# Expert up products with weight blocks stationary and 128 tokens moving, and the routing weight moved into the token rows

## The chip, the cores and the metric

The kernel runs on one core of one Trainium2 chip. The metric is the device time of one execution in microseconds (us), and the figure quoted for a kernel is the median over its runs. The profile comes from one further execution of the same program; its span runs from the first to the last instruction.

## The reference

The network works on 4 sequences of 512 tokens, 2,048 tokens of width 128, in six steps: a feed-forward block, a causal attention with 16 heads, the feed-forward block again, a mixture of experts, a second attention, and the mixture of experts again. Everything is float32. Only the mixture of experts is touched here:

```
def _L1_ffn_ref(X, Wg, bg, W1, W2, W3):          # E = 8 experts, top S = 2, H = 512
    logits = einsum('btd,de->bte', X, Wg) + bg
    topv, topi = top_k(logits, S)
    w = softmax(topv, axis=-1)
    xs = X[:, :, None, :] * w[..., None]
    out = X
    for e in range(E):
        h = silu(einsum('btsd,dh->btsh', xs, W1[e])) * einsum('btsd,dh->btsh', xs, W3[e])
        y = einsum('btsh,hd->btsd', h, W2[e])
        out = out + where(topi == e, y, 0).sum(axis=2)
```

The routing weight `w` multiplies the token row before both up products, so it stands inside the silu and once more in the other factor.

## The kernel before

Matrix products run on TensorE in float16. Each float32 operand is split into a high and a low half, and a product is three matmuls (high by high, high by low, low by high), which `split_mm` issues. Each weight is scaled by `W_UP` = 64 before it is split.

A mixture of experts is the function `moe(m)`, written once in each engine's program: m = 0 follows the first attention, m = 1 the second. The 4,096 pairs of token and expert are sorted by expert into tiles of 128 rows, padded so that each tile has one expert. There are `ETILES` = 46 tiles in two halves of `HT` = 23. The loop `run_tiles` goes over iterations t = 0 to 48 and calls up to four stages in each, with lags 0, 1, 2 and 3, and then `carried(m, t)`. The stages of tile t:

- Lag 0. GpSimd has fetched the tile's 128 token rows from memory with an indirect DMA (`gather`, L883) into `XG`, a ring of `XRING` = 4 buffers; the buffer is free again once TensorE has transposed it. TensorE transposes the rows (`turned_token`, L2130) into PSUM bank 0, ScalarE writes the high half (`token_high`, L1153), VectorE the low half (`token_low`, L1699).
- Lag 1. TensorE makes the two up products (`up`, L1746 to L1748, through `split_mm`): the token halves are stationary and 512 columns of the expert's weights move. The result stands tokens by hidden units in bank 1 (W1) and bank 2 (W3). ScalarE applies silu with the tile's row weights `wup` as scale (`gate`, L1161). VectorE multiplies the other product by `wup` and by the silu into `G32` (`product`, L1709).
- Lag 2. TensorE transposes the four 128 by 128 blocks of `G32` (`turned_product`, L2155) into bank 3 or 4, because the down product needs hidden units on the partitions. ScalarE writes the high half `GH` (`product_high`, L1167), VectorE the low half `GL` (`product_low`, L1715).
- Lag 3. TensorE makes the down product with twelve matmuls (`down`, L2167 to L2169): a 128 by 128 block of `GH` or `GL` is stationary, 128 columns of the expert's `E2` move. ScalarE scales the result (`result`, L1175), and GpSimd scatters the rows to memory (`scatter`, L891), eight iterations behind its gathers (`OUT_LAG` = 8).

Which expert a tile belongs to is known only at run time. TensorE's program reads the offsets of eight tiles at a time from SBUF into registers (`load_offsets`, called behind `up` at iterations that come five times in each `moe` after the start), and the address of each weight slice is worked out in registers: `ds(e, H)` in `up`, `ds(e + f * D, D)` in `down`, for the high and the low weights.

`carried(m, t)` puts other work between the tiles: the last turn of the attention ahead of them, for m = 0 the end of the second feed-forward block, the routing of the second half of the tokens (`routed`), for m = 0 transposes of the second attention's weights (`second_turned`, L2063), and the first turn of the next attention. Every engine works through its own program in order. `GRING` = 3 is the number of buffers of `GH` and `GL`.

Of the kernel before, what the change touches and what calls it, by code (L numbers as in the profile page):

```python
# [31 lines left out]
def macaron_block(nc: bass.Bass, ins, out, phases):  # L32
    tokens = ins["L0_attn_tokens"]
    NB, SEQ, D = tokens.shape
    P = 128
# [32 lines left out]
    with ctx:  # L68
# [296 lines left out]

        s_t_ps = sem("t_ps")
# [6 lines left out]
        s_gt_ps = sem("gt_ps")  # L373
# [7 lines left out]
        s_act_done = sem("act_done")  # L381

# [525 lines left out]
        def _(act):  # L908
# [237 lines left out]
            def moe(m):  # L1146
# [8 lines left out]
                def gate(t, w):  # L1155
                    if t % HT == 0:
                        act.wait_ge(s_r_weight, PARTS * m + t // HT + 1)
                    act.wait_ge(s_a_ps, w + 1)
                    if t >= 2:
                        act.wait_ge(s_g32_rdy, w - 1)  # L1160
                    a_.activation(SA[:, t % 2, :], ps[:, 1, :], ACT.Silu, scale=wup[:, t:t + 1]).then_inc(s_a_sb, 1)  # L1161

                def product_high(t, w):
                    act.wait_ge(s_gt_ps, w + 1)
                    if t >= GRING:
                        act.wait_ge(s_y_ps, w - GRING + 1)
                    a_.activation(GH[:, t % GRING].rearrange("p a b -> p (a b)"), ps[:, 3 + t % 2, :], ACT.Copy  # L1167
# [28 lines left out]
        def _(dve):  # L1196
# [389 lines left out]
            def homes_half(m, h):  # L1586
# [16 lines left out]
                v_.tensor_scalar(wup[:, at], wrow, 1.0 / W_UP, None, ALU.mult).then_inc(s_r_weight, 1)  # L1603
# [91 lines left out]
            def moe(m):  # L1695

                def token_low(t, w):
                    dve.wait_ge(s_t_hi, w + 1)
                    v_.tensor_tensor(XTt[:, t % 2, 1], ps[:, 0, 0:P], XTt[:, t % 2, 0], ALU.subtract  # L1699
                                     ).then_inc(s_t_lo, 1)  # L1700

                def product(t, w):
                    if t % HT == 0:
                        dve.wait_ge(s_r_weight, PARTS * m + t // HT + 1)
                    dve.wait_ge(s_a_sb, w + 1)
                    dve.wait_ge(s_b_ps, w + 1)
                    if t >= 2:
                        dve.wait_ge(s_gt_ps, w - 1)
                    v_.scalar_tensor_tensor(G32[:, t % 2, :], ps[:, 2, :], wup[:, t:t + 1], SA[:, t % 2, :], ALU.mult,  # L1709
                                            ALU.mult).then_inc(s_g32_rdy, 1)  # L1710

                def product_low(t, w):
                    g = t % GRING
                    dve.wait_ge(s_g_hi, w + 1)
                    v_.tensor_tensor(GL[:, g].rearrange("p a b -> p (a b)"), ps[:, 3 + t % 2, :],  # L1715
# [19 lines left out]
        def _(pe):  # L1735
# [376 lines left out]
            def moe(m):  # L2112
# [13 lines left out]
                def turned_token(t, w):  # L2126
                    pe.wait_ge(s_xg_in[t % XRING], moved(m, t % XRING, t + 1))
# [4 lines left out]
                def up(t, w):  # L2132
                    k, e = t % 2, offsets[t]
                    pe.wait_ge(s_t_lo, w + 1)
                    if t >= 1:
                        pe.wait_ge(s_a_sb, w)
                    split_mm(ps[:, 1, :], XTt[:, k, 0], XTt[:, k, 1], E1h[:].rearrange("p e h -> p (e h)")[:, ds(e, H)],
                             E1l[:].rearrange("p e h -> p (e h)")[:, ds(e, H)], s_a_ps)
                    if t >= 1:
# [57 lines left out]
```

## Time and profile before

| | us |
|---|---|
| median of 3 runs | 949.98 (949.64 to 950.70) |
| the profiled execution, its own time | 951.23 |
| its span | 949.4 |
| TensorE busy | 846.3 (89%) |
| VectorE busy | 788.4 (83%) |
| GpSimd busy | 744.6 (78%) |
| ScalarE busy | 646.6 (68%) |

TensorE is PE in the rows, its weight loads PEld, VectorE DVE, ScalarE ACT and GpSimd POOL. Instructions of TensorE overlap, so their durations add up to more than the time they take; what a matmul takes in a stream is the distance from one start to the next. Register arithmetic, register loads and waits are not shown as instructions. The two mixtures of experts run from about 357 to 508 us and from about 801 to 938 us of the span.

### The profile page before, as it was taken

To read this page: it belongs to the slowest core of one execution; us is meant where nothing else is said; L and a number is where in the kernel's file an instruction comes from. 1 tells how busy PE (TensorE), PEld (TensorE's weight loads), DVE (VectorE), ACT (ScalarE), POOL (GpSimd) and SP (SyncE) were. 2 spreads that over 40 slices of the span, in tenths; PEclk is the share of its full clock that TensorE was granted. 3 is DMA by queue.
4 is the path that set the end of the run, shared out by engine and by line. 5 is a ranking of instruction groups with operands and counts; after the bars stand their busy time and mean duration, and the time that the engine had idled before them with its cause. 6 is when DMAs were issued, how large, how long until landed. Compare 5 with 4: busy or idle time off the path is not lost.

```text
span 949.4 us, 32967 instructions
## 1 busy us (share of the span) xinstructions
PE 846.3 (89%) x12648; PEld 598.3 (63%) x12648; DVE 788.4 (83%) x2498; ACT 646.6 (68%) x1119; POOL 744.6 (78%) x685
## 2 busy tenths in 40 slices
PE   5779999999999867999997889999999995999994
PEld 3356675676666655776764566676777774576673
DVE  6769999989999976897776799898999987786673
ACT  6658797888787745766774667776676763566662
POOL 6849999999898956776653899988898985677762
PEclk9889999999999998999997999999999997999997
DMA  5122423242422341223111222133322231122232
GB/s 161 46 62 42 91 50 87 48 96 47 92 47 46 53 124 37 66 51 93 49 35 62 30 41 47 41 64 52 53 58 53 53 63 43 49 48 52 95 72 84
DMA packets 123516, 58.92 MB, mean 62 GB/s; under 512 B 106978, under 2 KB 112866, under 8 KB 123364
## 3 DMA queue, kind: packets, MB, share of 16 engines
q1 hardware_dynamic: 116128, 43.68, 21.3%
q0 software_dynamic: 5888, 12.07, 5.1%
q8 instruction: 106, 1.74, 0.8%
q10 hardware_dynamic: 1348, 1.05, 0.4%
q14 instruction: 46, 0.38, 0.2%
HBM read 22.44 MB, written 9.18 MB: 33 GB/s over the span
## 4 chain that ended last, share of the span: by engine, by line
PE 49%; DVE 19%; POOL 18%; issue 5%; ACT 5%; DMA 3%; SPq 0%; POOLq 0%; DVEq 0%; ACTq 0%
POOL arena L832 11%; PE ps L1746 6%; PE ps L1748 6%; PE ps L1747 6%; DVE ps L1347 5%; PE ps L1925 5%; PE ps L2155 4%; POOL arena L830 3%; PE ps L1899 2%; PE ps L2168 2%; PE ps L2167 2%; PE ps L2169 2%; PE ps L1958 2%; DVE arena L1371 1%; DMA T<-arena 1%
## 5 line engine op out<-in xcount | busy, mean ns | idle before, releaser
L832 POOL TENSOR_TENSOR arena<-arena 128x1024 f16<-128x1024 f32 x190 | 347.2, 1828 | 61.3 <-ACT arena L1028 51.3
L1020 ACT ACTIVATE arena<-ps,lift 128x1024 f32<-128x1024 f32 (+1 forms) x192 | 187.2, 975 | 114.4 <-PE ps L1935 103.9
L1347 DVE CUSTOM_DVE_ANT_0 ps<-ps,mask_qk 128x512 f32<-128x512 f32 (+3 forms) x512 | 238.6, 517 | 15.3 <-PE ps L1899 14.3
L1925 PE MATMUL ps<-arena 64*128 64x512 f16 (+3 forms) x1536 | 149.0, 299 | 13.9 <-ACT arena L1020 10.5
L883 POOL DMA_INDIRECT arena<-x_rows,arena x92 | 90.9, 989 | 57.0 <-PE ps L2130 21.9
L1958 PE MATMUL ps<-arena 128*128 128x65 f16 x1280 | 124.8, 195 | 5.5 <-DVE arena L1366 2.1
L1958 PEld LDWEIGHTS ps<-arena 128*128 128x128 f16 x1280 | 116.1, 97 | 18.8 <-issue 12.2
L891 POOL DMA_INDIRECT y_rows<-arena x92 | 91.0, 989 | 43.5 <-issue 22.7
L1959 PE MATMUL ps<-arena 128*128 128x64 f16 x1280 | 124.2, 193 | 0.0
L1960 PE MATMUL ps<-arena 128*128 128x65 f16 x1280 | 123.8, 193 | 0.0
L1959 PEld LDWEIGHTS ps<-arena 128*128 128x128 f16 x1280 | 117.3, 99 | 0.3 <-issue 0.3
L1960 PEld LDWEIGHTS ps<-arena 128*128 128x128 f16 x1280 | 117.3, 98 | 0.0
L830 POOL CAST arena<-arena 128x1024 f16<-128x1024 f32 x124 | 103.0, 831 | 0.0
L1925 PEld LDWEIGHTS ps<-arena 64*128 64x128 f16 x1536 | 55.0, 94 | 62.3 <-ACT arena L1020 34.8
L1709 DVE SCALAR_TENSOR_TENSOR arena<-ps,arena 128x512 f32<-128x512 f32 x92 | 68.8, 748 | 25.2 <-ACT arena L1161 23.4
L1899 PE MATMUL ps<-arena 64*128 64x512 f16 (+3 forms) x512 | 68.3, 304 | 21.1 <-DVE arena L1347 19.1
L1167 ACT ACTIVATE arena<-ps 128x512 f16<-128x512 f32 x92 | 54.9, 597 | 40.6 <-PE ps L2155 40.6
L1161 ACT ACTIVATE arena<-ps,arena 128x512 f32<-128x512 f32 x92 | 63.2, 687 | 27.7 <-PE ps L1748 26.7
L1715 DVE TENSOR_TENSOR arena<-ps,arena 128x512 f16<-128x512 f32 x92 | 63.3, 688 | 20.3 <-ACT arena L1167 19.8
L1347 DVE DVE_READ_ACCUMULATOR2_ANT arena<- 128x1 f16 x512 | 73.1, 143 | 0.0
L1354 DVE SCALAR_TENSOR_TENSOR arena<-ps,arena 128x512 f16<-128x512 f32 x64 | 43.8, 684 | 31.7 <-ACT arena L1041 31.7
L2167 PE MATMUL ps<-E2h,arena 128*128 x368 | 67.3, 219 | 1.8 <-ACT arena L1175 1.1
(283 smaller groups left out, 2609.7 us busy)
## 6 DMA issues: line engine op xcount, KB each, us to landing
stage<-in_L_ffn_W SPq DMA_DIRECT2D x4, 1024.0 KB, 5.6
arena<-y_rows SPq DMA_DIRECT2D x14, 256.0 KB, 3.8
x_rows<-XN SPq DMA_DIRECT2D x8, 256.0 KB, 2.3
arena<-x_rows,arena POOLq DMA_INDIRECT x92, 3.0
y_rows<-arena POOLq DMA_INDIRECT x92
stage<-in_L_attn_Wkv SPq DMA_DIRECT2D x2, 512.0 KB, 8.5
arena<-arena SPq DMA_TRANSPOSE x64, 2.3
T<-arena SPq DMA_TRANSPOSE x64, 3.1
```

The lines of the kernel that those rows point to most:

```text
L830: g.tensor_copy(PH[:, b, :, cols], P32[:, :, cols]).then_inc(s_ph_pool, 1)
L832: g.tensor_tensor(PL[:, b, :, cols], P32[:, :, cols], PH[:, b, :, cols], ALU.subtract).then_inc(s_pl, 1)
L883: g.indirect_dma_start(XG[:, t % XRING, :], None, x_rows[t // HT], bass.IndirectOffsetOnAxis(ap=row_i[:, 0, t:t + 1], axis=0)).then_inc(s_ ...
L891: g.indirect_dma_start(y_rows, bass.IndirectOffsetOnAxis(ap=row_i[:, 1, t:t + 1], axis=0), YS[:, t % YRING, :], None).then_inc(s_y_out[t % ...
L1020: a_.activation(P32[:, :, UNIT_AT[u]:UNIT_AT[u] + UNIT_W[u]], ps[:, 4:6, 0:UNIT_W[u]], ACT.Exp, bias=lift[:]).then_inc(s_ex_p, 1)
L1347: v_.tensor_tensor_reduce(ps[:, 2 + x, at:at + w], ps[:, 2 + x, at:at + w], mask_qk[:, CH - w:CH], 1.0, NEG, ALU.add, ALU.max, accum_out=M ...
L1899: ins_ = mm(ps[:, 2 + x, at:at + (i + 1) * P], QKh[rows, r, 0, i * P:(i + 1) * P], QKh[rows, r, 1, 0:(i + 1) * P], start=(n_ == 0), stop=( ...
L1925: mm(ps[:, 4 + x, at:at + w], keys, queries, start=(n_ == 0 and part == 0), stop=False)
L1958: mm(ps[:, bank, c:c + DH + 1], ph_, VH[:, r, k, x, 0:DH + 1], start=(k == 0), stop=False)
L1959: mm(ps[:, bank, c:c + DH], ph_, VL[:, r, k, x, :], start=False, stop=False)
L1960: ins_ = mm(ps[:, bank, c:c + DH + 1], pl_, VH[:, r, k, x, 0:DH + 1], start=False, stop=(k == i))
L2167: mm(dst, GH[:, g, f, :], wh, start=(f == 0), stop=False)
```

## The change

The up products are turned round. Blocks of 128 by 128 weights are now stationary and the 128 tokens of the tile move, so the result comes out as hidden units by tokens, four blocks side by side in a bank, and `turned_product` is gone. A row weight would then lie along the free dimension of the product, so it is multiplied into the token rows instead, before their transpose, by a new VectorE instruction (`scaled`). `wup` now holds the weight times `W_UP`. The two up products have two banks each (1 and 3, 2 and 4) in turn. `product_high` and `product_low` read `G32` in SBUF where they read the transposed copy in PSUM.

```diff
+        def a_bank(t):
+            return 1 + 2 * (t % 2)
+        def b_bank(t):
+            return 2 + 2 * (t % 2)
...
 # ScalarE
                 def gate(t, w):
-                    if t % HT == 0:
-                        act.wait_ge(s_r_weight, PARTS * m + t // HT + 1)
                     act.wait_ge(s_a_ps, w + 1)
...
-                    a_.activation(SA[:, t % 2, :], ps[:, 1, :], ACT.Silu, scale=wup[:, t:t + 1]).then_inc(s_a_sb, 1)
+                    a_.activation(SA[:, t % 2, :], ps[:, a_bank(t), :], ACT.Silu, scale=1.0 / (W_UP * W_UP)).then_inc(s_a_sb, 1)
                 def product_high(t, w):
-                    act.wait_ge(s_gt_ps, w + 1)
+                    act.wait_ge(s_g32_rdy, w + 1)
...
-                    a_.activation(GH[:, t % GRING].rearrange("p a b -> p (a b)"), ps[:, 3 + t % 2, :], ACT.Copy
+                    a_.activation(GH[:, t % GRING].rearrange("p a b -> p (a b)"), G32[:, t % 2, :], ACT.Copy
                                   ).then_inc(s_g_hi, 1)
...
 # VectorE
-                v_.tensor_scalar(wup[:, at], wrow, 1.0 / W_UP, None, ALU.mult).then_inc(s_r_weight, 1)
+                v_.tensor_scalar(wup[:, at], wrow, W_UP, None, ALU.mult).then_inc(s_r_weight, 1)
...
+                def scaled(t):
+                    if t % HT == 0:
+                        dve.wait_ge(s_r_weight, PARTS * m + t // HT + 1)
+                    dve.wait_ge(s_xg_in[t % XRING], moved(m, t % XRING, t + 1))
+                    xg = XG[:, t % XRING, :]
+                    v_.tensor_scalar(xg, xg, wup[:, t:t + 1], None, ALU.mult).then_inc(s_xg_scaled, 1)
...
                 def token_low(t, w):
+                    if t == 0:
+                        scaled(0)
                     dve.wait_ge(s_t_hi, w + 1)
                     v_.tensor_tensor(XTt[:, t % 2, 1], ps[:, 0, 0:P], XTt[:, t % 2, 0], ALU.subtract
                                      ).then_inc(s_t_lo, 1)
+                    if t + 1 < ETILES:
+                        scaled(t + 1)
 
                 def product(t, w):
...
                     if t >= 2:
-                        dve.wait_ge(s_gt_ps, w - 1)
-                    v_.scalar_tensor_tensor(G32[:, t % 2, :], ps[:, 2, :], wup[:, t:t + 1], SA[:, t % 2, :], ALU.mult,
-                                            ALU.mult).then_inc(s_g32_rdy, 1)
+                        dve.wait_ge(s_g_lo, w - 1)
+                    v_.scalar_tensor_tensor(G32[:, t % 2, :], ps[:, b_bank(t), :], 1.0 / (W_UP * W_UP), SA[:, t % 2, :],
+                                            ALU.mult, ALU.mult).then_inc(s_g32_rdy, 1)
 
                 def product_low(t, w):
                     g = t % GRING
                     dve.wait_ge(s_g_hi, w + 1)
-                    v_.tensor_tensor(GL[:, g].rearrange("p a b -> p (a b)"), ps[:, 3 + t % 2, :],
+                    v_.tensor_tensor(GL[:, g].rearrange("p a b -> p (a b)"), G32[:, t % 2, :],
                                      GH[:, g].rearrange("p a b -> p (a b)"), ALU.subtract).then_inc(s_g_lo, 1)
...
 # TensorE
                 def turned_token(t, w):
-                    pe.wait_ge(s_xg_in[t % XRING], moved(m, t % XRING, t + 1))
+                    pe.wait_ge(s_xg_scaled, w + 1)
...
                 def up(t, w):
                     k, e = t % 2, offsets[t]
                     pe.wait_ge(s_t_lo, w + 1)
-                    if t >= 1:
-                        pe.wait_ge(s_a_sb, w)
-                    split_mm(ps[:, 1, :], XTt[:, k, 0], XTt[:, k, 1], E1h[:].rearrange("p e h -> p (e h)")[:, ds(e, H)],
-                             E1l[:].rearrange("p e h -> p (e h)")[:, ds(e, H)], s_a_ps)
-                    if t >= 1:
-                        pe.wait_ge(s_g32_rdy, w)
-                    split_mm(ps[:, 2, :], XTt[:, k, 0], XTt[:, k, 1], E3h[:].rearrange("p e h -> p (e h)")[:, ds(e, H)],
-                             E3l[:].rearrange("p e h -> p (e h)")[:, ds(e, H)], s_b_ps)
+                    for bank, wh, wl, free, ready in ((a_bank(t), E1h, E1l, s_a_sb, s_a_ps),
+                                                      (b_bank(t), E3h, E3l, s_g32_rdy, s_b_ps)):
+                        if t >= 2:
+                            pe.wait_ge(free, w - 1)
+                        for f in range(HB):
+                            at = ds(e + f * P, P)
+                            split_mm(ps[:, bank, f * P:(f + 1) * P], wh[:].rearrange("p e h -> p (e h)")[:, at],
+                                     wl[:].rearrange("p e h -> p (e h)")[:, at], XTt[:, k, 0], XTt[:, k, 1],
+                                     ready if f == HB - 1 else None)
...
-                def turned_product(t, w):
-                    k = t % 2
-                    pe.wait_ge(s_g32_rdy, w + 1)
-                    if t >= 2:
-                        pe.wait_ge(s_g_lo, w - 1)
-                    for f in range(HB):
-                        ins_ = nc.tensor.transpose(ps[:, 3 + k, f * P:(f + 1) * P], G32[:, k, f * P:(f + 1) * P], ident[:])
-                    ins_.then_inc(s_gt_ps, 1)
...
-                run_tiles(m, (turned_token, up, turned_product, down), carried)
+                run_tiles(m, (turned_token, up, None, down), carried)
```

## Rows read from the trace of the kernel before

**Rows 1.** Busy time by stage; columns: PE, PEld, DVE, ACT, POOL, PEclk, DMA share.

```profile
397.00:434.00 37.00, 35.16 (x349) 25.34 (x345) 32.97 (x103) 22.96 (x53) 28.14 (x28) 1.00 0.22 51
845.00:928.00 83.00, 80.68 (x737) 57.98 (x735) 57.84 (x115) 54.03 (x126) 58.47 (x60) 1.00 0.27 69
```

**Rows 2.** The chain that ended last, 840 to 940 us, by line.

```profile
by line: PE ps L2155 16.1%; PE ps L1746 15.6%; PE ps L1747 15.1%; PE ps L1748 15.1%; PE ps L2168 8.3%; PE ps L2167 8.1%; PE ps L2169 7.8%; DMA arena<-y_rows 4.6%; PE ps L2130 4.3%; issue 3.4%; DMA y_rows<-arena 2.2%; POOL y_rows L891 1.0%; 
```

**Rows 3.** Timeline of PE, one tile of the second mixture; start, duration, line.

```profile
856.12 0.28 PE L2130 MATMUL ps<-ident,arena 128*128 128x128 f32 x1
856.24 0.38 PE L1746 MATMUL ps<-E1h,arena 128*128 x1
...
857.53 0.60 PE L2155 MATMUL ps<-ident,arena 128*128 128x128 f32 x4
857.97 0.22 PE L2167 MATMUL ps<-E2h,arena 128*128 x1
...
858.64 0.28 PE L2130 MATMUL ps<-ident,arena 128*128 128x128 f32 x1
```

**Rows 4.** Timeline of PEld: token transposes of tiles 4 and 45, both mixtures.

```profile
374.31 0.14 PEld L2130 LDWEIGHTS ps<-ident,arena 128*128 128x128 f32 x1
...
497.12 0.14 PEld L2130 LDWEIGHTS ps<-ident,arena 128*128 128x128 f32 x1
...
817.23 0.14 PEld L2130 LDWEIGHTS ps<-ident,arena 128*128 128x128 f32 x1
...
927.69 0.14 PEld L2130 LDWEIGHTS ps<-ident,arena 128*128 128x128 f32 x1
```

**Rows 5.** Timeline of PEld: a down product that follows a wait.

```profile
503.04 0.10 PEld L2167 LDWEIGHTS ps<-E2h,arena 128*128 128x128 f16 x1 [0.56 <-issue]
...
503.30 0.10 PEld L2167 LDWEIGHTS ps<-E2h,arena 128*128 128x128 f16 x1
503.39 0.10 PEld L2168 LDWEIGHTS ps<-E2l,arena 128*128 128x128 f16 x1
503.42 0.10 PEld L2169 LDWEIGHTS ps<-E2h,arena 128*128 128x128 f16 x1
503.54 0.10 PEld L2167 LDWEIGHTS ps<-E2h,arena 128*128 128x128 f16 x1
...
503.95 0.10 PEld L2169 LDWEIGHTS ps<-E2h,arena 128*128 128x128 f16 x1
```

**Rows 6.** Timeline of PEld behind a reload of the offsets.

```profile
871.06 0.42 PEld L2155 LDWEIGHTS ps<-ident,arena 128*128 128x128 f32 x4 [1.26 <-issue]
...
872.21 0.10 PEld L2169 LDWEIGHTS ps<-E2h,arena 128*128 128x128 f16 x1
872.30 0.14 PEld L2130 LDWEIGHTS ps<-ident,arena 128*128 128x128 f32 x1
872.55 0.10 PEld L1746 LDWEIGHTS ps<-E1h,arena 128*128 128x128 f16 x1
```

**Rows 7.** Timeline of POOL, 894 to 898 us.

```profile
894.39 0.97 POOL L883 DMA_INDIRECT arena<-x_rows,arena  x1 [0.30 <-PE ps L2130]
895.66 0.99 POOL L891 DMA_INDIRECT y_rows<-arena  x1 [0.30 <-issue]
896.96 0.97 POOL L883 DMA_INDIRECT arena<-x_rows,arena  x1 [0.30 <-PE ps L2130]
```

**Rows 8.** Timelines of DVE and POOL around 410 us.

```profile
409.77 1.22 DVE L1538 TENSOR_TENSOR arena<-row_no,arena 128x1024 f16<-128x1024 f16 x1
...
410.12 1.71 POOL L883 DMA_INDIRECT arena<-x_rows,arena  x1 [0.30 <-issue]
```

**Rows 9.** The page's lines of VectorE's low half and of a gather's landing.

```profile
L1715 DVE TENSOR_TENSOR arena<-ps,arena 128x512 f16<-128x512 f32 x92 | 63.3, 688 | 20.3 <-ACT arena L1167 19.8
...
arena<-x_rows,arena POOLq DMA_INDIRECT x92, 3.0
```

**Rows 10.** Busy time, 510 to 520 us, in the columns of the first group.

```profile
510.00:520.00 10.00, 7.17 (x47) 3.19 (x47) 6.00 (x22) 3.52 (x6) 1.27 (x2) 0.63 0.38 118
```

More of the change, by code:

```diff
@@ L364, in macaron_block @@
         s_xg_in = [sem("xg_in0"), sem("xg_in1"), sem("xg_in2"), sem("xg_in3")]
+        s_xg_scaled = sem("xg_scaled")
         s_t_ps = sem("t_ps")
@@ L372, in macaron_block @@
         s_g32_rdy = sem("g32_rdy")
-        s_gt_ps = sem("gt_ps")
         s_g_hi = sem("g_hi")
@@ L1700, in token_low @@
                                      ).then_inc(s_t_lo, 1)
+                    if t + 1 < ETILES:
+                        scaled(t + 1)
                 def product(t, w):
-                    if t % HT == 0:
-                        dve.wait_ge(s_r_weight, PARTS * m + t // HT + 1)
                     dve.wait_ge(s_a_sb, w + 1)
```

## Prediction

> **What bounds the kernel now.** I read the page's chain first. It is spread over the whole network, and only the two mixtures of experts are touched, so I went to the busy times by stage. In the plain stretch of the second mixture PE is busy 80.68 of 83 us and no other engine above 58.47 [rows 1]. The chain of that stretch is PE almost alone: the product transposes of L2155 hold 16.1% of it, the up products 46%, the down product 24% [rows 2]. The timeline then gives one tile: token transpose 0.12 us, up products from 856.24 to 857.53, 1.29 us, product transposes 0.44, down product 0.67, together 2.52 us from one token transpose to the next [rows 3]. GpSimd is hardly slower a bound: gather and scatter follow each other at 1.27 and 1.30, 2.57 us a tile [rows 7]. From the token transpose of tile 4 to that of tile 45 it takes 122.8 us in the first mixture and 110.5 in the second, 41 tiles each, 3.00 and 2.69 us a tile [rows 4]. What lies above 2.52 is carried work and the reloads of the offsets. In the routing stretch of the first mixture DVE is busy 32.97 of 37 us and bounds along with PE [rows 1].
>
> **What the change removes from PE.** The four transposes, 0.44 us a tile, and the wait for `G32` ahead of them. Six matmuls of 512 columns become 24 of 128. In the down product a matmul of 128 columns with a weight load of its own takes (858.64 - 857.97) / 12 = 0.056 us [rows 3], so 24 take 1.34 in place of 1.29. Array time falls from 2.52 to 0.12 + 1.34 + 0.67 = 2.13 us a tile. Here a rule of the Trainium skill speaks against the change ("TensorE: Matmul & The Clock Gate", section on the back-to-back issue gap): in a real kernel a stream of weight loads and 128-column matmuls is put at about 81 ns each. By it the 24 would take 1.94 us and the tile, down product included, about 3.0. The 0.056 us row disagrees, and I do not use the rule.
>
> **What it adds to PE's program, and this decides.** A weight slice's address depends on the tile's expert and is worked out in registers between the matmuls. In the plain tile this costs nothing, because the six long up matmuls let PE's program run ahead of the array. One place shows its own pace: the down product behind a wait at 503.04 us, with nothing issued ahead. The loads of a group of three start 0.12 us, 0.09 and 0.03 apart (503.42 to 503.54, 503.30 to 503.39, 503.39 to 503.42): a new offset `e + f * D` with the address of the high slice, then the address of the low slice, then a load whose address is known. A group takes 0.24 us where the array needs 0.17, and the first eleven steps of the twelve loads take 0.91 [rows 5]. Behind a reload of the offsets the pace shows again: 0.09 from the last load of a down product to the token transpose and 0.25 from there to the first up load [rows 6].
>
> After the change the tile has 12 such groups in place of 4, and no long matmul behind which they could be issued. I sum its issue: token transpose 0.09; first up group 0.25 + 0.09 + 0.03 = 0.37; the other seven 0.24 each if every `e + f * P` is worked out anew, 0.21 if one that is already known is used again (0.09 + 0.09 + 0.03), 1.47 to 1.68; the down product's first group, behind its waits, 0.27, the other three 0.63 to 0.72. That makes 2.83 to 3.13 us; I take 3.0. It is above the array's 2.13, GpSimd's 2.57 and what DVE needs for a tile, so PE's issue sets the pace. Nothing hides it.
>
> **The sum.** 41 tiles at 3.0 are 123.0 us in each mixture. Five reloads of the offsets: each shows as 1.26 us without a load [rows 6]; between nothing more and 1.3 is on the path, I take 1.2, so 6.0. Carried matmuls are issued at 0.03 each: in the second mixture the routing's 65, 2.0 us; in the first mixture about 190, 5.7, and 3.0 us of array time that issue does not cover. This last is an estimate: the next attention's first turn has six matmuls of 512 columns at 1.29 / 6 = 0.215 and twelve of 128 at 0.056, 2.0 us, the feed-forward's down products 64 of 128, 3.6 us; they lie in three iterations, each of which covers 3.0 - 2.13 = 0.87. Second mixture: 131.0 against 110.5, 20.5 more. First: 137.7 against 122.8, 14.9 more. The first four tiles wait on the attention's end, and behind tile 45 three iterations lose the transposes and gain issue; I put both at nothing, within 1 us either way. Together 35.4. The profiled execution took 951.23 us (its span of 949.4 and 1.8 around it), 1.25 above the median of the runs; 951.2 + 35.4 = 986.6, and on the scale of the runs 985.4. I say 985.
>
> **The other edits.** `scaled` adds one DVE instruction a tile. None of its kind and size is in these rows. The nearest is the low half of 512 columns, 0.69 us [rows 9]; a quarter of it, 0.17, is the lower bound, 0.97 the upper, if it must wait out a whole GpSimd instruction [rows 7]. I take 0.3, near the shorter end, as it has 128 columns: 12 us of DVE in each mixture, inside the 0.5 us that the tile gets longer. It also puts the landing of a gather (3.0 us [rows 9]) into DVE's queue ahead of `product` and `product_low`; at 3.0 us a tile the gathers run ahead and the wait is empty. If PE were as fast as its array, DVE would wait there in every tile. `gate` and `product` change a scale only; `product_high` reads as many elements from SBUF; both at nothing. The second set of banks lets `up` start two tiles ahead of its readers, which PE doesn't need while it issues late.
>
> **Rivals.** *GpSimd's pace, faster.* If address work were hidden (say the eight new groups cost no more than their matmuls), gathers and scatters would set 2.57 us a tile. Issue decides from 2.57 us on. Second mixture: 41 x 2.57 = 105.4, 5.1 less, and about 6 less at the end, since a token transpose would follow its gather by the landing's 3.0 us instead of trailing by the ring. First mixture: the routing stretch stays with DVE, the plain 21 tiles give some 6. That is 17 less, 933 us. For it speaks that PE is now the longest queue; against it the 0.24 us group.
>
> *The shared reader.* A gather that began at 410.12 us, while a DVE instruction with two SBUF inputs ran, lasted 1.71 us instead of 0.97, and that DVE instruction ended at 410.99 [rows 8]. `product_low` (0.69 us [rows 9]) gets two SBUF inputs, once a tile. Where GpSimd bounds, each tile could lose up to about 0.33: 2.9 us a tile, which eats most of the 17, 947 us. At 3.0 us a tile GpSimd has 0.4 to spare, and it costs nothing. The Trainium skill says the same of this pair ("SBUF — State Buffer", rules on the shared port pair: a VectorE instruction with two SBUF inputs blocks a GpSimd instruction that reads SBUF); the row agrees, with 0.74 us lost once.
>
> *The slow clock.* PE's granted clock is 1.00, its upper level (2.4 GHz), in both stretches [rows 1], and 0.63 at 510 us, where PE waits for whole microseconds [rows 10]. A late issue makes many short gaps, not long ones. If the clock fell to its lower level (1.2 GHz), the 36 short matmuls would take 0.111 each, 4.2 us a tile: 82 tiles by 1.2 more, about 1,085 us.
>
> **How the numbers follow.** Issue bound 0.74, GpSimd's pace 0.14, GpSimd with the shared reader 0.06, slow clock 0.04, something without effect 0.02. The likeliest case's own range is 968 to 1,006: 2.83 to 3.13 us a tile is 14 us down and 11 up, and reloads and carried work are 6 us either way. To hold 8 in 10 the range must take in the shared reader's 947, and it leaves out the fast rival and the slow clock: 945 to 1,008. About 0.2% is what a measurement of this kernel can tell from no change. Faster by more than that: 0.18 (the fast rival and most of the shared reader's). Within it: 0.03. Slower: 0.79.
>
> **What the changed profile would show.** Right: no L2155; in the plain stretch a token transpose every 2.9 to 3.1 us; weight loads of the up products 0.12, 0.09 and 0.03 apart, not 0.056 even; "issue" high in the chain; DVE, ACT and POOL each with idle time in every tile; POOL waiting for L2130 before its gathers. The fast rival would show loads 0.056 apart and POOL without a wait, 2.57 us a tile, with DVE idle ahead of `scaled` until the gather lands. The shared reader would show scatters or gathers of 1.1 to 1.6 us. The prediction falls if address work costs the array nothing when the weights are the stationary side, or if fewer addresses are worked out than I counted.

## The result and the profile after

The changed kernel takes 1006.19 us (median of 5 runs, 1001.9 to 1010.58) against 949.64 for the kernel before in the same session; the ratio is 1.0607, with a 95% interval of 1.0577 to 1.0637. A second comparison, in a later session, gave 1.0605 (1.0582 to 1.0629). The change makes the kernel slower by 6%. The profiled execution took 1010.58 us, its span is 1008.7; the spans are 949.4 and 1008.7, 59.3 apart; the medians are 56.5 apart.

In the kernel after, L2145 is the token transpose, L1761 to L1763 the three matmuls of a group in `up`, L2174 to L2176 those of `down`, L891 the gather and L899 the scatter; on VectorE L1708 is `scaled`, L1714 `token_low`, L1724 `product` and L1730 `product_low`, on ScalarE L1167 is `gate` and L1181 `result`.

The token transposes of tiles 4 and 45 after, in the timeline of PE's weight loads, against those of [rows 4]:

```profile
376.24 0.14 PEld L2145 LDWEIGHTS ps<-ident,arena 128*128 128x128 f32 x1
...
523.18 0.14 PEld L2145 LDWEIGHTS ps<-ident,arena 128*128 128x128 f32 x1
...
845.21 0.14 PEld L2145 LDWEIGHTS ps<-ident,arena 128*128 128x128 f32 x1
...
986.34 0.14 PEld L2145 LDWEIGHTS ps<-ident,arena 128*128 128x128 f32 x1
```

The 41 tiles take 146.9 us in the first mixture and 141.1 in the second, 24.1 and 30.7 more than [rows 4]. That is 54.8 of the 59.3 us. The rest, 4.5, lies outside these stretches (1.9 of it ahead of tile 4 of the first mixture, 1.9 between the mixtures).

Busy time by stage after: both stages of the first mixture, both of the second, and the plain tiles alone; columns as in [rows 1].

```profile
400.00:441.00 41.00, 39.64 (x504) 32.51 (x503) 34.13 (x113) 19.41 (x49) 26.13 (x26) 1.00 0.19 42
441.00:523.20 82.20, 73.98 (x872) 62.57 (x871) 51.15 (x115) 43.02 (x104) 44.41 (x46) 0.96 0.18 49
...
878.00:986.30 108.30, 100.66 (x1171) 82.31 (x1168) 62.15 (x146) 48.74 (x124) 59.32 (x60) 0.97 0.21 53
886.00:908.90 22.90, 22.73 (x264) 18.24 (x262) 12.58 (x29) 10.95 (x28) 13.72 (x14) 1.00 0.20 43
```

A reader who stops here sees a PE that is busy 22.73 of 22.90 us in the plain tiles and may take the array for the bound. The chain of these tiles says the same, with nearly nothing under "issue" (critical chain, 886 to 909 us):

```profile
by line: PE ps L1761 30.8%; PE ps L1763 15.1%; PE ps L2175 14.9%; PE ps L1762 13.6%; PE ps L2174 12.8%; PE ps L2176 7.3%; PE ps L2145 4.9%; issue 0.7%
```

It isn't the array. A matmul's busy time in this trace runs from its start to its end, and the 36 short ones overlap; how closely they follow each other can only be read from the loads. DVE is busy 55% of these tiles, ACT 48%, POOL 60%: all three wait, and PE waits for none of them (its matmuls show no wait at all from 886 to 909 us). This is one plain tile (892.56 to 895.78 us, 3.22 us) in the timeline of the loads; left out are the groups that look like their neighbours.

```profile
892.56 0.14 PEld L2145 LDWEIGHTS ps<-ident,arena 128*128 128x128 f32 x1
892.81 0.10 PEld L1761 LDWEIGHTS ps<-arena,E1h 128*128 x1
892.82 0.10 PEld L1762 LDWEIGHTS ps<-arena,E1h 128*128 x1
892.97 0.10 PEld L1763 LDWEIGHTS ps<-arena,E1l 128*128 x1
893.11 0.10 PEld L1761 LDWEIGHTS ps<-arena,E1h 128*128 x1
893.13 0.10 PEld L1762 LDWEIGHTS ps<-arena,E1h 128*128 x1
893.20 0.10 PEld L1763 LDWEIGHTS ps<-arena,E1l 128*128 x1
893.35 0.10 PEld L1761 LDWEIGHTS ps<-arena,E1h 128*128 x1
...
894.62 0.10 PEld L1763 LDWEIGHTS ps<-arena,E3l 128*128 x1
894.84 0.10 PEld L2174 LDWEIGHTS ps<-E2h,arena 128*128 128x128 f16 x1
894.97 0.10 PEld L2175 LDWEIGHTS ps<-E2l,arena 128*128 128x128 f16 x1
895.01 0.10 PEld L2176 LDWEIGHTS ps<-E2h,arena 128*128 128x128 f16 x1
...
895.68 0.10 PEld L2176 LDWEIGHTS ps<-E2h,arena 128*128 128x128 f16 x1
895.78 0.14 PEld L2145 LDWEIGHTS ps<-ident,arena 128*128 128x128 f32 x1
```

A group of three starts every 0.24 us (893.11 to 893.35), where the array needs 0.17. The loads of L1761 and L1763, each with an address of its own, come late (0.14 to 0.15 and 0.07 us behind the load before them); that of L1762, on the address that L1761 has just used, comes 0.01 to 0.02 us behind it. The seven tiles from 886.08 to 908.9 take 3.25 us each.

Around a reload of the offsets the same view shows, for the down product's first load and the ones behind it:

```profile
910.90 0.10 PEld L1763 LDWEIGHTS ps<-arena,E3l 128*128 x1
913.20 0.10 PEld L2174 LDWEIGHTS ps<-E2h,arena 128*128 128x128 f16 x1 [2.21 <-issue]
```

2.30 us in place of the 0.22 of a plain tile (894.62 to 894.84). Before the change it was 1.26 without a load [rows 6]. Behind this one the clock is at its lower level (1.2 of 2.4 GHz) for most of the next 4.2 us (granted clock 0.59 in the second row; busy time by stretch, the columns as above):

```profile
911.00:913.30 2.30, 0.21 (x4) 0.10 (x1) 1.29 (x2) 0.36 (x1) 0.70 (x1) 1.00 0.19 61
913.30:917.50 4.20, 4.20 (x46) 4.10 (x46) 0.70 (x3) 1.61 (x4) 1.96 (x2) 0.59 0.07 19
```

The engines' waits in the plain tiles, 886 to 909 us (total, times, longest), say who waits for whom:

```profile
DVE arena L1724 <- ACT arena L1167: 8.5, 7, 1.3
POOL arena L891 <- PE ps L2145: 6.8, 7, 1.5
ACT arena L1181 <- PE ps L2176: 6.7, 7, 1.1
ACT arena L1167 <- PE ps L1763: 5.1, 7, 0.8
```

POOL waits about 1 us for the token transpose before each gather, in seven of seven tiles; before the change the gathers of [rows 7] begin 0.30 us behind the scatter, the distance that stands between any two starts, and so do 19 of the 22 gathers from 850 to 908 us (0.30 to 0.36).

### The profile page after: what moved, and what is told of

It is laid out like the page before. It is cut to its first block, busy times and chain, and to the rows that moved or that the text cites. A ratio compares the mean times of both kernels' runs of the same rounds, so it can differ in the third digit from the quotient of the medians.

```text
span 1008.7 us, 36649 instructions
## 1 busy us (share of the span) xinstructions
PE 892.3 (88%) x13936; PEld 665.0 (66%) x13936; DVE 801.6 (79%) x2590; ACT 633.1 (63%) x1119; POOL 755.1 (75%) x685
## 4 chain that ended last, share of the span: by engine, by line
PE 55%; POOL 18%; DVE 14%; issue 5%; ACT 5%; DMA 2%; SPq 0%; POOLq 0%; ACTq 0%; DVEq 0%
POOL arena L840 11%; PE ps L1761 11%; PE ps L1763 7%; PE ps L1762 6%; PE ps L1940 5%; DVE ps L1353 4%; PE ps L2175 4%; PE ps L2174 3%; POOL arena L838 3%; PE ps L1914 2%; PE ps L2176 2%; PE ps L1973 2%; PE ps L1974 2%; PE ps L1975 2%; PE ps L2145 1%
## 5 line engine op out<-in xcount | busy, mean ns | idle before, releaser
L891 POOL DMA_INDIRECT arena<-x_rows,arena x92 | 95.8, 1042 | 101.0 <-PE ps L2145 71.1
L899 POOL DMA_INDIRECT y_rows<-arena x92 | 92.5, 1006 | 49.0 <-ACT arena L1181 25.2
L1724 DVE SCALAR_TENSOR_TENSOR arena<-ps,arena 128x512 f32<-128x512 f32 x92 | 63.5, 691 | 65.2 <-ACT arena L1167 58.2
L2174 PE MATMUL ps<-E2h,arena 128*128 x368 | 80.2, 220 | 18.8 <-DVE arena L1730 12.6
L1181 ACT ACTIVATE arena<-ps 128x128 f32<-128x128 f32 x92 | 25.5, 278 | 99.7 <-PE ps L2176 99.7
L1167 ACT ACTIVATE arena<-ps 128x512 f32<-128x512 f32 x92 | 54.9, 597 | 52.7 <-PE ps L1763 52.5
L1761 PE MATMUL ps<-arena,E1h 128*128 128x128 f16 x368 | 81.2, 230 | 0.3
L2176 PE MATMUL ps<-E2h,arena 128*128 x368 | 80.8, 221 | 0.0
L1761 PE MATMUL ps<-arena,E3h 128*128 128x128 f16 x368 | 80.5, 222 | 0.2
```

Of the source, the lines that this page charges most:

```text
L891: g.indirect_dma_start(XG[:, t % XRING, :], None, x_rows[t // HT], bass.IndirectOffsetOnAxis(ap=row_i[:, 0, t:t + 1], axis=0)).then_inc(s_ ...
L1761: mm(dst, sh, mh, start=True, stop=False)
L2174: mm(dst, GH[:, g, f, :], wh, start=(f == 0), stop=False)
L2176: ins_ = mm(dst, GL[:, g, f, :], wh, start=False, stop=(f == HB - 1))
```

## The experiments

Twelve kernels ran in three sessions, four to a session. The kernel before took 989.52 us in the first (984.84 to 991.52, 9 runs), 948.8 in the second and 949.33 in the third. Four kernels of the first session were therefore run once more; a ratio stands beside the kernel before of its own session. The times in us that the first session's expectations name were set from 949.6, and all four came out above them. The expectations call this "another chip". That was my guess, and the record doesn't bear it out: the first and the last session carry the same chip number. The pairs are told together.

**Up weights at fixed addresses.** Expert 0's weights are used for all up products, so the eight up groups need no address work; the down product keeps its addresses.

```diff
-                            at = ds(e + f * P, P)
+                            at = slice(f * P, (f + 1) * P)
```

> The changed kernel with the weight slices of both up products at fixed addresses: every tile multiplies with expert 0's W1 and W3, which changes what is computed; the down product keeps its expert. The 24 matmuls, their stationary weights and their sizes stay. Issue theory: without the 16 addresses a tile's up products fall to the array's 8 x 0.17 us, the tile to about 0.25 + 1.34 + 0.1 + 0.94 = 2.6 to 2.75 us, close to GpSimd's 2.57; the time comes down to 935 to 950 us. Rival, stationary weight blocks are slow by themselves (80 ns for each load and 128-column matmul instead of 56): the tile stays at 3.1 us or above and the time above 990. Rival, the wait for the scaled rows: stays above 1,000.

> The changed kernel with the up weights at fixed addresses (always expert 0), a second time. Theory, PE's address work sets the pace: without the addresses of the up products the tile falls to GpSimd's pace, 2.6 us, and the ratio to the kernel before lies below 1.00 (0.98). First run of it: ratio 1.007 with tiles between 2.12 and 4.9 us and gaps of 0.4 to 0.7 us between matmuls that wait for nothing. If those gaps are the chip's (another chip, or a chance state), they are gone and 0.98 comes. If they belong to the number of instructions, which is as high here as in the changed kernel, they come again at the same ratio, 1.00 to 1.01, and half of the loss of the change is not the arithmetic but the supply of instructions.

Measured first 996.04 us, ratio 1.0068 (1.004 to 1.0096); again 943.45 us, ratio 0.9929 (0.9905 to 0.9954). In the second run the loads follow each other at the array's pace, and tiles of 2.12 to 2.16 us appear where PE doesn't wait:

```profile
891.89 0.10 PEld L1761 LDWEIGHTS ps<-arena,E1h 128*128 128x128 f16 x1
891.93 0.10 PEld L1762 LDWEIGHTS ps<-arena,E1h 128*128 128x128 f16 x1
891.99 0.10 PEld L1763 LDWEIGHTS ps<-arena,E1l 128*128 128x128 f16 x1
892.04 0.10 PEld L1761 LDWEIGHTS ps<-arena,E1h 128*128 128x128 f16 x1
```

The chain that ended last, 850 to 915 us, by line, is no longer PE's:

```profile
by line: POOL y_rows L899 31.2%; POOL arena L891 31.0%; issue 20.8%; DMA arena<-x_rows,arena 5.9%; PE ps L1761 2.1%; PE ps L1763 2.1%; PE ps L1762 2.1%; PE ps L2175 1.5%; PE ps L2176 1.4%; PE ps L2174 1.3%; PE ps L2145 1.1%; DVE arena L1708
```

and DVE waits ahead of the scaling for the gather to land (waits, 850 to 908 us):

```profile
DVE arena L1708 <- DMA arena<-x_rows,arena: 7.5, 10, 2.1
```

Taking the address work of the eight up groups away is thus worth 1.0605 - 0.9929, 6.8% of the kernel before, or some 64 us, and behind it stands GpSimd's pace, as the fast rival had it. The first run also had gaps of its own. In its timeline of loads:

```profile
897.55 0.10 PEld L1762 LDWEIGHTS ps<-arena,E1h 128*128 128x128 f16 x1
898.13 0.10 PEld L1763 LDWEIGHTS ps<-arena,E1l 128*128 128x128 f16 x1 [0.48 <-issue]
898.18 0.10 PEld L1761 LDWEIGHTS ps<-arena,E1h 128*128 128x128 f16 x1
```

No wait, no address and no reload stands between these loads. The same kernel shows none of this in the second run, so it belongs to that session and not to the kernel. A supply of instructions that came late would look like this; no run shows that it was that.

**The kernel before, with short up matmuls.** Each up matmul of 512 columns becomes four of 128, the tokens stay the stationary side. Once with an address for each weight block, and once at expert 0's fixed addresses.

```diff
-                    split_mm(ps[:, 1, :], XTt[:, k, 0], XTt[:, k, 1], E1h[:].rearrange("p e h -> p (e h)")[:, ds(e, H)],
-                             E1l[:].rearrange("p e h -> p (e h)")[:, ds(e, H)], s_a_ps)
+                    for f in range(HB):
+                        split_mm(ps[:, 1, f * P:(f + 1) * P], XTt[:, k, 0], XTt[:, k, 1],
+                                 E1h[:].rearrange("p e h -> p (e h)")[:, ds(e + f * P, P)],
+                                 E1l[:].rearrange("p e h -> p (e h)")[:, ds(e + f * P, P)], s_a_ps if f == HB - 1 else None)
```

(E3 likewise; with fixed addresses `f * P:(f + 1) * P` stands for `ds(e + f * P, P)`.)

> The kernel before, with each up product cut into four blocks of 128 weight columns: tokens stay stationary and weights move, transposes and routing weights as before, but there are 24 matmuls of 128 columns with 16 register addresses, as in the changed kernel. Issue theory: the tile goes from 2.52 to about 3.3 to 3.5 us (3.22 of the changed kernel and the transposes' issue), the time to 1,005 to 1,030 us. Rival, it is the weights as stationary side that is slow: array time alone, 2.52 + 0.05 a tile, 950 to 957 us.

> The kernel before with each up matmul of 512 columns cut into four of 128, tokens the stationary side as before, the addresses of the 16 weight blocks a tile worked out from the tile's offset: the counterpart to the same cut at fixed addresses, which gave 1.003. Theory: what costs is the address work, whichever side the weights are; six groups more than the kernel before has (8 in place of 2) bring the tile from 2.52 to 3.3 us and more, ratio 1.04 to 1.06. Rival: addresses cost the array only where they are those of the stationary side; then the ratio is that of the fixed addresses, 1.00.

> The kernel before with each up matmul of 512 columns cut into four of 128 (tokens stay the stationary side) and all of them at fixed addresses (expert 0), so that they need no address work. The same cut with addresses gave a ratio of 1.049. Theory, address work sets the pace: without it the 24 short matmuls take as long as the array needs, 1.34 us in place of 1.29, and the ratio is 1.00 (0.995 to 1.01). Rival, the number of instructions: 24 loads and matmuls in place of 6 cost nearly the same with or without addresses, ratio 1.02 or more, with gaps inside plain sequences.

With addresses: 1036.55 us, ratio 1.0489 (1.0449 to 1.053), and again 1019.06 us, ratio 1.0731 (1.0705 to 1.0758). At fixed addresses: 952.18 us, ratio 1.0034 (1.0018 to 1.005). This pair is the cleanest of the study: the same number of matmuls of the same shapes in the same order, with and without addresses, each beside the kernel before of its own session. (I had expected 1.04 to 1.06 with addresses; it came out above.) One group of each in the timeline of loads, with addresses:

```profile
887.03 0.10 PEld L1746 LDWEIGHTS ps<-E1h,arena 128*128 128x128 f16 x1
887.19 0.10 PEld L1747 LDWEIGHTS ps<-E1l,arena 128*128 128x128 f16 x1
887.22 0.10 PEld L1748 LDWEIGHTS ps<-E1h,arena 128*128 128x128 f16 x1
887.33 0.10 PEld L1746 LDWEIGHTS ps<-E1h,arena 128*128 128x128 f16 x1
```

and at fixed ones:

```profile
881.95 0.10 PEld L1746 LDWEIGHTS ps<-E1h,arena 128*128 128x128 f16 x1
882.01 0.10 PEld L1747 LDWEIGHTS ps<-E1l,arena 128*128 128x128 f16 x1
882.06 0.10 PEld L1748 LDWEIGHTS ps<-E1h,arena 128*128 128x128 f16 x1
882.12 0.10 PEld L1746 LDWEIGHTS ps<-E1h,arena 128*128 128x128 f16 x1
```

0.30 us for this group (0.20 to 0.27 for the other seven of the tile) against 0.17. A plain tile takes 3.34 us with addresses (token transposes at 886.54 and 889.88) and 2.57 without (881.67 and 884.24): 0.77 us for the addresses of eight groups, 0.19 of it already between the token transpose and the first up load (0.25 against 0.06). Without addresses the 24 short matmuls cost 0.05 us a tile more than six long ones (2.57 against [rows 3]'s 2.52), which is the prediction's 1.34 in place of 1.29. Here the product transposes are still there and the tokens are stationary, yet the kernel is as slow as the changed one and slower. So neither the stationary side nor the number of matmuls is what costs; the number of addresses is. Whether it is the arithmetic in registers or the instruction that carries a computed address was not separated; that L1762 follows L1761 by 0.01 to 0.02 us speaks for the arithmetic.

**Without the scaling.** The token rows are not multiplied by the routing weight at all, and the token transpose waits for the gather.

```diff
-                    xg = XG[:, t % XRING, :]
-                    v_.tensor_scalar(xg, xg, wup[:, t:t + 1], None, ALU.mult).then_inc(s_xg_scaled, 1)
...
-                    pe.wait_ge(s_xg_scaled, w + 1)
+                    pe.wait_ge(s_xg_in[t % XRING], moved(m, t % XRING, t + 1))
```

> The changed kernel without the VectorE instruction that scales the token rows: the routing weights are left out of the computation, and TensorE waits for the gathers themselves. Issue theory: TensorE's pace does not depend on it, 1,000 to 1,010 us. Rival, the scaled rows come late and hold the token transpose: faster by 10 us or more.

> The changed kernel without the scaling of the token rows, a second time (the routing weights are left out of the products, and the token transpose waits for the gather itself). Theory: PE's issue sets the pace and the scaling is hidden in DVE's idle time, so nothing comes back but some of the first mixture's routing stretch, where DVE is nearly full: ratio to the kernel before 1.05 to 1.06, a plain tile 3.2 us as with it. Rival: the scaling, which stands ahead of the product in DVE's queue, costs a good part of the loss; the first run on another chip gave 1.032, and by the rival that comes again, with about 0.3 us less in each tile.

Measured first 1019.53 us, ratio 1.0317 (1.0278 to 1.0357); again 1005.45 us, ratio 1.0594 (1.0571 to 1.0618), beside 1.0605 (1.0582 to 1.0629) with the scaling. From tile 4 to 45 it takes 146.0 and 141.1 us, with it 146.6 and 141.2. The scaling is hidden, in the first mixture too to within 0.6 us. The first run's 1.0317 has a slow kernel before below it (989.52) and is no gain: by itself this kernel took 14 us longer then than in the third session.

**One offset at a time.** The same edit in the changed kernel (twice) and in the kernel before: instead of eight offsets in every eighth tile, PE reads one in each tile, three tiles ahead.

```diff
-                        tile_ei[0:1, t:min(t + 8, HT * (t // HT + 1))], engines=(mybir.EngineType.PE,), min_val=0,
+                        tile_ei[0:1, t:t + n], engines=(mybir.EngineType.PE,), min_val=0,
...
-                    if t % HT % 8 == 5 and t % HT + 3 < HT:
-                        load_offsets(t + 3)
+                    if t % HT + 3 < HT:
+                        load_offsets(t + 3, 1)
```

> The changed kernel reading one tile's offset at a time, three tiles ahead, behind every up product, in place of eight at a time. A reading of eight held TensorE 2.3 us in the changed kernel. If the cost goes by the value (0.28 us each), the total stays within 10 us of the changed kernel, 1,000 to 1,015 us. If it goes by the reading (2 us each, about 84 of them in place of 12), 1,130 us or more.

> The changed kernel with the offsets read one by one, three tiles ahead, the edit that gained 0.7% in the kernel before. Theory: with PE's own program as the bound there is nothing behind which a reading hides, so it costs what eight values cost, an eighth at a time (2.3 / 8 = 0.29 us), and the ratio stays at 1.06 (1.055 to 1.07), a plain tile at 3.5 us. Rival: as in the kernel before, a short reading hides where a long one doesn't; then five times 2.3 us come back in each mixture and the ratio is 1.04.

> The kernel before with the experts' offsets read one by one, three tiles ahead, in place of eight at a time in every eighth tile. Theory, a reading costs by the value (0.28 us each): PE's program runs ahead of the array by the length of the long up matmuls, so that 0.28 us a tile hides where 2.3 us every eighth tile doesn't, and the ten readings' 1.2 us each come back: ratio 0.988. If a reading costs the same for one value as for eight, or the tile has no slack left, 84 readings make the kernel slower, ratio 1.02 or more.

In the changed kernel: 1026.52 us in a single run, and again 1019.49 us, ratio 1.0732 (1.0703 to 1.076). In the kernel before: 942.37 us, ratio 0.9927 (0.9908 to 0.9946). In the changed kernel the reading stands open in every tile, between the last up load and the first down load:

```profile
889.23 0.10 PEld L1763 LDWEIGHTS ps<-arena,E3l 128*128 x1
889.85 0.10 PEld L2174 LDWEIGHTS ps<-E2h,arena 128*128 128x128 f16 x1 [0.53 <-issue]
```

0.62 us here and 0.58 in the next tile (892.93 to 893.51), 0.22 without it: some 0.36 to 0.40 for one value where eight cost 2.1 (2.30 - 0.22), 0.26 each. My 0.29 was low by a quarter, and so the ratio rose above the changed kernel's own, and above the 1.055 to 1.07 expected. In the kernel before the same reading is not seen. Busy time, 845 to 920 us, of the kernel before and then of this one:

```profile
845.00:920.00 75.00, 72.68 (x666) 52.12 (x663) 52.33 (x105) 48.61 (x113) 54.96 (x57) 1.00 0.27 69
```

```profile
845.00:920.00 75.00, 75.00 (x677) 54.25 (x675) 53.33 (x98) 50.81 (x119) 54.62 (x57) 1.00 0.28 72
```

PE is busy all of the 75 us and its waits are empty. Tile 4 to 45 takes 120.3 and 107.5 us, 2.5 and 3.0 less than [rows 4]. I had expected 12 us in all and 6.4 came: three of the second mixture's five reloads had shown as 1.1 us each (tiles of 3.64, 3.62 and 3.49 against 2.52), the two among carried matmuls as 0.4 at most. This kernel keeps the arithmetic of the one before, leaves nothing out, and is faster than both kernels of the comparison (0.7% faster than the one before).

**The product kept in PSUM,** on top of fixed up addresses. `product` writes over its PSUM bank, both halves read it there, and the bank is free a step later.

```diff
-                    v_.scalar_tensor_tensor(G32[:, t % 2, :], ps[:, b_bank(t), :], 1.0 / (W_UP * W_UP), SA[:, t % 2, :],
+                    v_.scalar_tensor_tensor(ps[:, b_bank(t), :], ps[:, b_bank(t), :], 1.0 / (W_UP * W_UP), SA[:, t % 2, :],
...
-                    v_.tensor_tensor(GL[:, g].rearrange("p a b -> p (a b)"), G32[:, t % 2, :],
+                    v_.tensor_tensor(GL[:, g].rearrange("p a b -> p (a b)"), ps[:, b_bank(t), :],
...
-                                                      (b_bank(t), E3h, E3l, s_g32_rdy, s_b_ps)):
+                                                      (b_bank(t), E3h, E3l, s_g_lo, s_b_ps)):
```

> The changed kernel with the up weights at fixed addresses (0.993), and the product kept in its PSUM bank instead of SBUF, so that the low half of the product has one SBUF input in place of two. With fixed addresses GpSimd sets the pace. Theory, the shared reader: gathers and scatters that begin while the low half runs are held up (means of 1.07 us where the kernel before has 0.99); with one SBUF input they come back to 0.99, 2 x 0.07 us a tile, some 12 us over both mixtures, unless another queue binds first: ratio 0.98 to 0.985. Rival: what stretches them is something else (traffic of the transfers), and the ratio stays at 0.993; PSUM banks that come free later could eat a gain.

Measured 941.56 us, ratio 0.9909 (0.9877 to 0.9941); its interval overlaps that with the product in SBUF, so for the whole kernel the comparison is inconclusive, and the 0.98 to 0.985 that the theory asked for didn't come. The mechanism shows in the rows. GpSimd's starts, 380 to 920 us (count, busy, mean ns), with the product in SBUF:

```profile
L899 POOL DMA_INDIRECT y_rows<-arena x84 | 89.5, 1066 | 32.1 <-issue 22.2 <-ACT arena L1181 9.9
L891 POOL DMA_INDIRECT arena<-x_rows,arena x83 | 88.4, 1065 | 35.7 <-issue 21.8 <-DVE arena L1563 9.1 <-PE ps L2145 4.8
```

and in PSUM:

```profile
L899 POOL DMA_INDIRECT y_rows<-arena x86 | 86.0, 999 | 33.6 <-issue 22.7 <-ACT arena L1181 10.6 <-PE ps L2145 0.3
L891 POOL DMA_INDIRECT arena<-x_rows,arena x83 | 82.2, 991 | 40.3 <-issue 16.9 <-PE ps L2145 13.4 <-DVE arena L1563 10.0
```

The means fall by 0.07 us, as expected. Sorting the starts by what VectorE does at that moment shows whose they are: with the product in SBUF the 45 starts that fall into a low half (L1730) take 1.20 us on average and the other 122 take 1.02; with it in PSUM the 42 that fall into one take 0.98, the others 1.00. In the kernel before, where the low half also has one SBUF input, 55 such starts take 0.97. One such case with the product in SBUF: the low half ran on DVE from 894.14 to 894.82 us, and the scatter that began in it took 1.34 us instead of 0.99.

```profile
894.34 1.34 POOL L899 DMA_INDIRECT y_rows<-arena  x1 [0.30 <-issue]
```

In the second mixture tile 4 to 45 goes from 109.4 to 105.9 us, which is close to 41 times GpSimd's 2.57 (105.4); its starts there stand 0.30 us apart without a break from 846 to 903 us. But GpSimd is not alone: the chain that ended last, 850 to 915 us, is now mostly PE's, and PE waits 23 times for the low half that frees the bank, the price of keeping the product there:

```profile
PEld ps L1761 <- DVE arena L1730: 3.8, 23, 0.4
```

In the first mixture the time stays (119.8 and 120.2).

**The changed kernel once more,** beside the runs of the second session:

> The changed kernel, nothing altered, beside the next three runs. The times so far come from different chips (the kernel before takes 949.6 us on one and 989.5 us on another), so a row of one chip can't be set beside a row of the other. If the chip scales both kernels alike, the ratio to the kernel before is 1.06, as measured first, and about 3.2 us a tile. If the slower chip loses its time where instructions are short (many more of them in the changed kernel), the ratio rises above 1.07 and a plain tile needs 3.4 us or more.

1007.22 us, ratio 1.0605, and 146.6 and 141.2 us from tile 4 to 45, as in the first profile. The ratio is the first one again; nothing here speaks of short instructions that are dearer in one session than in another.

## Why the prediction was right, and where its sizes were off

**The direction and the bound were right.** The tile's array time fell, and PE's issue of computed addresses took its place. The case is shown from both sides: take the addresses away and the loss is gone (0.9929); put addresses into the old kernel and the loss is there without the change (1.0731). Fixed addresses there give 1.0034.

**The size was not.** The prediction said 985 us, 35.4 more than before; 1006.19 came, 56.5 more. It lies inside the stated 945 to 1,008 by 2 us, and that is in part luck. The range of the issue case alone was added up wrongly: 14 us down and 11 up, with 6 either way, is 965 to 1,002 around 985, not 968 to 1,006, and the measured time lies 4 us above it. Of the signs, PE's pace, POOL's wait for the token transpose and the idle time of the other engines came; a tile of 2.9 to 3.1 us did not (3.25), and "issue" is not high in the chain but 0.7%, because the modelled matmuls fill it.

**The tile, 3.0 us, measured 3.22 to 3.25.** This is the larger error, 9 to 10 us over 41 tiles. By the prediction's own steps, in the tile shown: token transpose 0.10 (said 0.09); first up group, from the token transpose's load to its third, 0.41 (0.37); the other seven 1.65 from 892.97 to 894.62, 0.236 each (1.47 to 1.68); the down product's first group 0.39 from 894.62 to 895.01 (0.27); its other three 0.67 (0.63 to 0.72). The sum is 3.22. Both of the prediction's prices occur among the seven groups: over the seven plain tiles the medians are 0.24 us for W1's and 0.20 to 0.23 for W3's, 1.60 together; short stray gaps bring their mean to 1.67, near the upper end. That W3's are cheaper because their offsets were worked out for W1 just before was not tested. The prediction names no row for the down group's 0.27; the group of [rows 5] that begins at 503.04 takes 0.26, and it was not preceded by the last up product's group. Of the 0.39, 0.22 pass before its first load. What fills them, waits or addresses, wasn't separated.

**A reload, 1.2 us, measured 2.3.** The step that failed is reading a price from a row with a cover over it. The 1.26 us of [rows 6] was what was left when PE's program had run ahead; I took that run-ahead away in the same prediction and kept the number. Tiles with a reload in the second mixture's plain part last 5.53, 5.51 and 5.15 us, 2.3, 2.3 and 1.9 above their neighbours (the last reads seven values, the other two eight: a half has 23 tiles); the two among carried matmuls show less, about 0.9 and 0.4. Together about 8 in place of 6.0 in that mixture. With 9 to 10 for the tile term that makes 11 to 12 us, and the mixture missed by 10.1 (141.1 against 131.0), so the carried matmuls there cost less than the 2.0 that was said. The first missed by 9.2 (146.9 against 137.7); the tile term alone is as large, so its reloads and its 8.7 us of carried work nearly cancel in their errors, and no run separates them. What the first four tiles and the ends do, put at nothing within 1 us, was 4.5 in all.

The Trainium skill says in "Runtime: NRT & Kernel Launch", section "Instruction fetch mechanics", that loading registers from HBM costs about 200 ns a register even in bulk. This load reads SBUF; the trace agrees in kind, with 0.26 us a value in a reading of eight and nearly 0.4 in a reading of one, above the page's figure in both.

**The other edits cost nothing,** as said: the scaling takes 277 ns on DVE in the plain tiles (said 0.3), and taking it out changes nothing (1.0594 against 1.0605).

**The fast rival and the shared reader were real but stood in the second row.** With addresses gone, GpSimd's pace and the wait for the gather's landing are there as described, at 943 us where the rival said 933. Of the missing 10 us, 3.5 to 4 are the second mixture's 109.4 against 105.4, by the run with the product in PSUM GpSimd's starts held up by the low half; the first mixture gave 3.0 in place of 6; behind tile 45 of the second came 1.3 us (20.4 in place of 21.7) where the rival had some 6. Its 0.33 us a tile for the shared reader was the price of one collision (1.34 against 0.99); a start that fell into a low half lost 0.2 on average, and spread over all starts it is 0.07.

**The slow clock** stayed a rival in small. Of the six reloads that stood open for 1.9 us or more, four were followed by 4.2 us at a granted clock of 0.59 to 0.73, two by none of it (1.00). At the lower level the groups start 0.32 us apart in place of 0.24 (914.90, 915.22, 915.54 us), the loads about 0.107. Yet the tile behind that reload (914.37 us, granted clock 0.63) took 3.28 us and the one after it 3.05, together less than two neighbours: PE's program ran ahead of the slow array, and the loads behind 916.81 us follow each other at 0.05 to 0.06. Where issue is the bound, a slow array costs little.

**What the gains became.** The product transposes' 0.44 us and the wait for `G32` are gone from PE, as planned. PE then had no long instruction left behind which its own program could run ahead, and paid 0.25 us ahead of the up products (0.12 before [rows 3]), 0.07 more a group, 0.39 for the down product's first group, and nearly every reload in full.

## What to carry to other kernels

Where TensorE's instructions take register-computed addresses it showed two speeds here, that of its array (0.17 us a group) and that of its own program (0.24); long instructions hid the second, and a change that turns six long ones into 24 short ones uncovered it, although array time fell. Before cutting instructions shorter, find a place in the trace where the engine runs with nothing issued ahead, read the spacing there, and price reloads and register reads at their full length and not at what was left open before. Where long instructions remained, small reads in every tile hid better than a large one in every eighth: that alone made the old kernel 0.7% faster (0.9927).

## What the runs showed that I had not expected

Reading one value into a register costs nearly 0.4 us where eight cost 2.1, so a part of it, some 0.1 by an estimate from these two, would be paid for each reading. Where PE's program has no cover, reading one by one is therefore worse (1.0732 against 1.0605).

A session in which the kernel before took 989.5 us instead of 949, with the same chip number as a later one at 949.3. In it, PE stood still for 0.4 to 0.7 us inside sequences without waits or addresses, and the kernels that PE's address work holds back lost less against their later runs (17 us for the kernel before with short matmuls, 14 without the scaling, 7 with one offset at a time) than the two that it doesn't (53 for fixed up addresses, 40 for the kernel before). Ratios taken in such a session mislead although their intervals are narrow (1.0317 then, 1.0594 later, for one kernel). What it was stays open; no run isolated it.

Short gaps of 0.07 to 0.2 us also appear at changing places inside groups of the changed kernel and its variants. They are in the 0.236 us a group that was measured, and their cause wasn't separated from the address work.
